# Running maxima stored by chunk and gathered by node, in the max pass of a four-layer graph network

## What is computed

```python
msgs = z[dst] @ Wd + z[src] @ Ws + edge_weight[:, None] * ww[None, :] + bm
agg = segment_max(msgs, dst)          # for each node, over its incoming edges
hidden = relu(z @ W1a + agg @ W1b + b1)
x = layernorm(z + hidden @ W2 + b2)
```

## Time and profile before

| | |
|---|---|
| median of three runs | 3843.29 us (3842.65, 3843.29, 3858.65) |
| span of the profiled execution | 3851.9 us (no other time of it is given) |
| busy in it: PE, DVE, ACT, POOL | 81%, 38%, 25%, 61% |
| first and last gather of the max pass | 1961.4 and 3185.4 us |
| granted TensorE clock over the span | 0.818 |

### The profile page before, as it was taken

The page is one execution under the profiler, slowest core; times in us unless marked ns, Lnnn a source line. Parts: engine busy times, 40 slices in busy tenths (PEclk is TensorE's granted clock), DMA queues, the critical chain, the costliest instruction groups (busy, mean ns, idle before and its releaser), DMA issues.

```text
span 3851.9 us, 54329 instructions
## 1 busy us (share of the span) xinstructions
PE 3125.2 (81%) x21070; PEld 2150.6 (56%) x21070; DVE 1459.7 (38%) x3223; ACT 958.7 (25%) x2512; POOL 2340.9 (61%) x2327
## 2 busy tenths in 40 slices
PE   3788788878889888888857787878878787999898
PEld 2444444455557677777735555555656564555454
DVE  6555555223222111111224444544444443333333
ACT  2555455122222011010122222322222232000000
POOL 3666662666662665666446666666666662777775
PEclk7899999899999999999955665665665667999899
DMA  5444444655555666666433343433444337666564
GB/s 150 162 160 166 167 149 156 200 175 185 190 181 172 193 193 188 198 193 201 144 112 103 108 116 101 119 102 112 112 127 127 111 113 253 211 226 218 195 225 144
DMA packets 278767, 621.83 MB, mean 161 GB/s; under 512 B 60077, under 2 KB 188649, under 8 KB 270953
## 3 DMA queue, kind: packets, MB, share of 16 engines
q1 hardware_dynamic: 171944, 372.56, 28.5%
...
## 4 chain that ended last, share of the span: by engine, by line
PE 56%; another core or an unknown queue 15%; issue 13%; DVE 7%; ACT 6%; DMA 3%; SPq 1%; DVEq 0%; POOL 0%; ACTq 0%; POOLq 0%
PE banks L2056 27%; PE banks L1294 5%; PE banks L2077 4%; PE banks L554 3%; PE banks L2075 3%; PE banks L1283 3%; PE banks L1272 3%; PE banks L1274 1%; PE banks L529 1%; PE banks L2170 1%; PE banks L1154 1%; DMA ring_of_rows<-weight_parts 1%; ACT arena L2363 1%; ACT arena L1213 1%
## 5 line engine op out<-in xcount | busy, mean ns | idle before, releaser
L2056 PE MATMUL banks<-arena 128*128 128x384 bf16 (+1 forms) x9310 | 1557.1, 316 | 129.0 <-issue 114.3
L2056 PEld LDWEIGHTS banks<-arena 128*128 128x128 bf16 x9310 | 914.4, 100 | 618.0 <-issue 235.8
L516 POOL DMA_INDIRECT arena<-tab_l,ring_of_rows x831 | 808.4, 973 | 472.3 <-issue 286.3
L2121 POOL DMA_INDIRECT arena<-h_pieces,span_sources x450 | 435.8, 968 | 319.2 <-issue 108.3
L2121 POOL DMA_INDIRECT ring_of_rows<-message_pieces,span_sources x396 | 430.2, 1086 | 214.1 <-issue 98.0
L2121 POOL DMA_INDIRECT ring_of_rows<-x_pieces,span_sources x306 | 332.9, 1088 | 201.3 <-PE banks L2075 101.1
L1294 PE MATMUL banks<-arena 128*128 128x64 f32 x1662 | 349.8, 380 | 123.4 <-issue 123.0
L2101 DVE TENSOR_TENSOR arena<-iota_bf,span_targets 128x768 bf16<-128x768 bf16 x243 | 134.9, 556 | 822.3 <-remote 318.3
L2121 POOL DMA_INDIRECT ring_of_rows<-l_pieces,span_sources x306 | 300.7, 983 | 233.0 <-issue 71.8
L1294 PEld LDWEIGHTS banks<-arena 128*128 128x128 f32 x1662 | 315.9, 284 | 201.5 <-issue 190.4
L1388 DVE TENSOR_TENSOR_SCAN ring_of_rows<-arena,ring_of_rows,banks 128x512 f32<-128x512 bf16 x207 | 264.2, 1277 | 135.6 <-remote 57.7
...
## 6 DMA issues: line engine op xcount, KB each, us to landing
...
arena<-scan_mask SPq DMA_DIRECT2D x208, 128.0 KB
...
arena<-tab_l,ring_of_rows POOLq DMA_INDIRECT x831
```

The source lines that it names most:

```text
L516: k.nc.gpsimd.indirect_dma_start(k.RG3[:, i % p.ring, at:at + width], None, table, bass.IndirectOffsetOnAxis(ap=k.SRC[:, i:i + 1], axis=0) ...
L2056: t = T.matmul(k.bank[i % N_SUMS][:, 0:rows.shape[-1]], counts[:, s, :], rows, start=s == 0 and n == 0, stop=s == NT - 1 and n == len(term ...
L2121: G.indirect_dma_start(k.rows[p.layer][s % n], None, k.pieces[p.layer], bass.IndirectOffsetOnAxis(ap=k.SRCG[:, at:at + 1], axis=0)).then_i ...
```

## The change

The one-hots, the selecting product and the copy of windows go. ACT now copies each turned-back chunk into one of four buffers, and SP stores it as 256 KB of DRAM, so that all running maxima lie there by edge. For each group of nodes POOL gathers the rows of the nodes' last edges from there, one indirect DMA for each tile of 128 nodes, into `BEST3`, nodes on partitions; a group's gathers stand eight chunks behind its last chunk, and behind waits for the stores of its last four chunks. Two new stages, "bturn" on PE and "bcopy" on ACT, turn them for "first". All stages of nodes move four chunks later. Turning back alternates between two banks. Which edge is a node's last is counted in the first layer: in each of the two steps of `vector_keys` two comparisons and two sums, then a few small operations (`vector_last_rows`), a small store, and at the start of `l1b` a load of 128 x 49 single words in place of the four arrays.

```diff
-HOT_RING = 3
+RUNS, NODE_CHUNKS, ROWS_AFTER = 4, 4, 8
+BACKS = (3, 0)
...
-    "l2": ("first", "relu", "second", "residual", *LN1, "xturn", "xcopy", "parts", "table", "parts2", "table2", *PIECES),
+    "l2": ("bturn", "bcopy", "first", "relu", "second", "residual", *LN1, "xturn", "xcopy", "parts", "table", "parts2", "table2",
+           *PIECES),
...
-PLACES_AT = 24
-PARKED = 2 + 5
+PARKED = 2 + 2
...
-            while done < end and (NEWEST[done] if regular else min(done, N_ET - 1)) < (c * CH if c < NCH else N_ET):
+            while done < end and (NEWEST[done] if regular else min(done, N_ET - 1)) < ((c - NODE_CHUNKS * regular) * CH if c < NCH else N_ET):
...
-def window(k, c):
-    return k.bank[c % 2][:, 0:WINDOW]
+def last_chunk(g):
+
+    return NEWEST[DONE_BY[g] - 1] // CH
+
+
+def runs_stored(k, c):
+
+    return k.sem(f"store_runs_{c % RUNS}"), 16 * (c // RUNS + 1)
+
+
+def node_rows(k, g):
+
+    return k.sem(f"node_rows_{g % 2}"), 16 * sum(GROUPS[g % 2:g + 1:2])
+
+
+def best_turned(k, g):
+    if g >= NG - 2:
+        return k.BEST_TURNED[g - NG + 3][:, 0:GROUPS[g] * P]
+    return k.BEST_TURNED[0][:, 0:GROUPS[g] * P]
 
 
 def max_tensor_l2(k, p):
     T = k.nc.tensor
 
     def node(stage, g):
-        if stage == "first":
-            T.wait_ge(*p.selected(g))
+        if stage == "bturn":
+            T.wait_ge(*node_rows(k, g))
             if g == 0:
                 T.wait_ge(k.sem("l2_folded"), 2)
             if before_group(g) >= 0:
                 T.wait_ge(*max_tabled(p, before_group(g)))
+            turn(k, g, lambda j: k.BEST3[:, j, :], H, (max_bank(g),), p.sem(stage))
+        elif stage == "first":
+            T.wait_ge(*p.at("bcopy", g))
             o = k.bank[max_bank(g)][:, 0:GROUPS[g] * P]
             T.matmul(o, k.w1_2[:, 0, :], k.ROWT3[:, gslice(g), :], start=True, stop=False)
-            T.matmul(o, k.w1_2[:, 1, :], k.BEST3[:, gslice(g), :], start=False, stop=True).then_inc(p.sem(stage), 1)
+            T.matmul(o, k.w1_2[:, 1, :], best_turned(k, g), start=False, stop=True).then_inc(p.sem(stage), 1)
...
-            T.matmul(bank[:, q * P:(q + 1) * P], k.RG3[:, i % p.ring, UP:UP + H], k.IDENT, is_transpose=True, start=i == tiles[0], stop=False)
+            T.matmul(bank[:, q * P:(q + 1) * P], k.LANDED[:, i % REGULAR_RING, :], k.IDENT, is_transpose=True, start=i == tiles[0], stop=False)
...
         T.wait_ge(k.sem("l2_scanned"), c + 1)
-        if c:
-            T.wait_ge(k.sem("l2_back_copied"), c)
+        if c >= 2:
+            T.wait_ge(k.sem("l2_back_copied"), c - 1)
         for q in range(len(chunk_tiles(c))):
-            t = T.transpose(k.bank[BACK][:, q * P:(q + 1) * P], k.SCAN[c % 2][:, q * P:(q + 1) * P], k.IDENT)
+            t = T.transpose(k.bank[BACKS[c % 2]][:, q * P:(q + 1) * P], k.SCAN[c % 2][:, q * P:(q + 1) * P], k.IDENT)
         t.then_inc(k.sem("l2_back"), 1)
-
-    def select(c):
-
-        T.wait_ge(p.hot, c + 1)
-        T.wait_ge(k.sem("l2_back_copied"), c + 1)
-        if c >= 2:
-            T.wait_ge(k.sem("l2_selected"), c - 1)
-        tiles = chunk_tiles(c)
-        for q, i in enumerate(tiles):
-            t = T.matmul(window(k, c), k.RG3[:, i % p.ring, 0:H], k.HOT[:, c % HOT_RING, q, :], start=i == tiles[0], stop=i == tiles[-1])
-        t.then_inc(p.product, 1)
...
-        if c:
-            select(c - 1)
...
-    select(NCH - 1)
...
-    def one_hots(c):
-
-        n = len(chunk_tiles(c))
-        if c >= HOT_RING:
-            V.wait_ge(p.product, c - HOT_RING + 1)
-        V.tensor_tensor(k.HOT[:, c % HOT_RING, 0:n, :], k.IOTA[:, 1:WINDOW + 1].unsqueeze(1).to_broadcast([P, n, WINDOW]),
-                        k.LOCEND[:, c * CH:c * CH + n].unsqueeze(2).to_broadcast([P, n, WINDOW]), ALU.is_equal).then_inc(p.hot, 1)
-
-    def take(c):
-
-        V.wait_ge(p.product, c + 1)
-        if c:
-            V.wait_ge(k.sem("l2_selected"), c)
-        if c % REGS == 0:
-            V.load(k.ve_regs, k.BASES[0:1, c:c + REGS])
-        V.tensor_copy(k.BEST[:, bass.ds(V.snap(k.ve_regs[c % REGS], min_val=0, max_val=N - 1), WINDOW)],
-                      window(k, c)).then_inc(k.sem("l2_selected"), 1)
...
-    V.memset(k.BEST[:, N:NP + WINDOW], 0.0).then_inc(k.sem("l2_acc_set"), 1)
-    V.wait_ge(k.sem("l2_acc_set"), 1)
     scan(0)
-    one_hots(0)
...
-            one_hots(c + 1)
...
-        if c:
-            take(c - 1)
-    take(NCH - 1)
...
+        if stage == "bcopy":
+            A.wait_ge(*p.at("bturn", g))
+            if before_group(g) >= 0:
+                A.wait_ge(*p.at("first", before_group(g)))
+            A.copy(best_turned(k, g), k.bank[max_bank(g)][:, 0:GROUPS[g] * P]).then_inc(p.sem(stage), 1)
...
-        n, slot = len(chunk_tiles(c)), c * CH % p.ring
+        n = len(chunk_tiles(c)) * P
         A.wait_ge(k.sem("l2_back"), c + 1)
-        if c * CH >= p.ring:
-            A.wait_ge(p.product, c - p.ring // CH + 1)
-        A.copy(k.RG3[:, slot:slot + n, 0:H], wide(k.bank[BACK][:, 0:n * P], P)).then_inc(k.sem("l2_back_copied"), 1)
+        if c >= RUNS:
+            A.wait_ge(*runs_stored(k, c - RUNS))
+        A.copy(k.MAXIMA[c % RUNS][:, 0:n], k.bank[BACKS[c % 2]][:, 0:n]).then_inc(k.sem("l2_back_copied"), 1)
...
+    def results(g):
+
+        if g >= 2:
+            G.wait_ge(*node_rows(k, g - 2))
+        for c in range(last_chunk(g) - RUNS + 1, last_chunk(g) + 1):
+            G.wait_ge(*runs_stored(k, c))
+        for j in gtiles(g):
+            G.indirect_dma_start(k.BEST3[:, j, :], None, k.runs_dram[0:last_chunk(g) + 1].rearrange("c p (q h) -> (c p q) h", h=H),
+                                 bass.IndirectOffsetOnAxis(ap=k.LAST[:, j:j + 1], axis=0)).then_inc(node_rows(k, g)[0], 16)
+
+    groups = list(range(NG))
     for i in range(N_ET):
+        if i % CH == 0:
+            while groups and i // CH >= last_chunk(groups[0]) + ROWS_AFTER:
+                results(groups.pop(0))
         if i >= AHEAD and i % CH == 0:
             G.wait_ge(k.sem("l2_turned"), (i - AHEAD) // CH + 1)
-        gather(k, p, i, k.tab["l2"], H, UP)
+        G.indirect_dma_start(k.LANDED[:, i % REGULAR_RING, :], None, k.tab["l2"],
+                             bass.IndirectOffsetOnAxis(ap=k.SRC[:, i:i + 1], axis=0)).then_inc(p.landed(i)[0], 16)
+    for g in groups:
+        results(g)
...
+    def store_runs(c):
+
+        S.wait_ge(k.sem("l2_back_copied"), c + 1)
+        S.dma_start(k.runs_dram[c], k.MAXIMA[c % RUNS]).then_inc(runs_stored(k, c)[0], 16)
...
+        if c:
+            store_runs(c - 1)
...
             first_slab(FIRST_SLAB_AT.index(c))
+    store_runs(NCH - 1)
     nodes(k.slots[NCH][0])
...
-    S.wait_ge(p.product, NCH)
+    for c in range(NCH - RUNS, NCH):
+        S.wait_ge(*runs_stored(k, c))
...
     V.scalar_tensor_tensor(k.WKEY[:, a:b, :], high, 2.0, rel, ALU.mult, ALU.add).then_inc(k.sem("win_keyed"), 1)
+    V.wait_ge(k.sem("win_keyed"), n + 1)
+    upto = k.WUPTO[:, 0:m].rearrange("p (s e) -> p s e", e=REC)
+    for r in range(2):
+        V.tensor_scalar(upto, rel, float(r), None, ALU.is_le).then_inc(o.sem, o.up())
+        V.wait_ge(o.sem, o.n)
+        V.tensor_reduce(k.WENDS[:, a:b, r], upto, AX_X, ALU.add).then_inc(o.sem, o.up())
+        V.wait_ge(o.sem, o.n)
+
+
+def vector_last_rows(k):
+
+    V, o = k.nc.vector, k.order
+
+    def settled():
+        V.wait_ge(o.sem, o.n)
+
+    def flat(v):
+        return v.rearrange("p s r -> p (s r)")
+
+    V.tensor_scalar(k.WFROM, k.WSTI[:, SPANS:SPANS + SETS], 2.0, -1.0, ALU.mult, ALU.add).then_inc(o.sem, o.up())
+    settled()
+    V.tensor_tensor(k.WLAST, k.WENDS, k.WFROM.unsqueeze(2).to_broadcast([P, SETS, 2]), ALU.add).then_inc(o.sem, o.up())
+    settled()
+    last, tile, at, chunk = flat(k.WLAST), k.WPARTS[0], k.WPARTS[1], k.WPARTS[2]
+    V.tensor_scalar(tile, last, 7, CH - 1, ALU.logical_shift_right, ALU.bitwise_and)
+    V.tensor_scalar(at, last, P - 1, 2, ALU.bitwise_and, ALU.logical_shift_left)
+    V.tensor_scalar(chunk, last, 9, 9, ALU.logical_shift_right, ALU.logical_shift_left).then_inc(o.sem, o.up())
+    settled()
+    V.tensor_tensor(at, at, tile, ALU.add).then_inc(o.sem, o.up())
+    settled()
+    V.tensor_tensor(chunk, chunk, at, ALU.add).then_inc(k.sem("last_rows"), 1)
...
     count_own(0)
+    vector_last_rows(k)
...
+            S.wait_ge(k.sem("last_rows"), 1)
+            S.dma_start(k.last_dram.rearrange("(s p f) -> p s f", p=P, f=4),
+                        k.WPARTS[2].rearrange("p (s f) -> p s f", f=4)).then_inc(k.sem("store_last_rows"), 16)
...
-    def places():
-
-        V.wait_ge(k.sem("park"), 16 * PARKED)
-        V.tensor_tensor(k.CHANGE, k.DST, k.NEXT, ALU.not_equal)
-        V.tensor_tensor(k.WITHIN, k.DST, k.FIRST, ALU.subtract).then_inc(o.sem, o.up())
-        V.wait_ge(o.sem, o.n)
-        V.scalar_tensor_tensor(k.LOCEND[:, 0:N_ET], k.WITHIN, 1.0, k.CHANGE, ALU.add, ALU.mult).then_inc(k.sem("l2_places"), 1)
...
```

(9 more changed lines are left out.)

19 lines of the change are left out of this document (10 added, 9 removed).

## The result

The changed kernel took 3906.23 us (median of 4 runs, 3895.66 to 3911.04) beside 3845.76 us (4 runs, 3842.65 to 3858.65): a ratio of 1.0136, 95% interval 1.0107 to 1.0166. It is slower by about 60 us where I forecast about 80 us less. The profiled execution's span is 3899.8 us, 47.9 us more than that of the kernel before.

What follows compares the result with a forecast made beforehand. The prediction took PE's work to bound the max pass, with POOL next. Pass -87, tail +2 and front +6 summed to -79 us, giving 3773 us in a profile and 3764 us as a median, range 3714 to 3818.

Steps and rivals of the forecast that it cites:

- the first reading: Max pass before the change: PE, idle 1.20 us of 5.97 a chunk, is nearest its limit and holds POOL up.
- the waits left on POOL: Max pass after the change: POOL still waits 25 us, bounds none or 168 us.
- the tail: From the last gather's end to the first load of messages: 34.3 us, not 32.7, so +2 us, bounds -3 and +8.
- the front: First layer's two key steps: extra comparisons, sums and small operations on DVE add 6 us, bounds 0 and 9.
- 875 gathers at 1.272 us: Max pass on POOL: 831 gathers plus 44 of last rows take 1113 us, against 1225 us for the pass before.
- Selection out of the chunk, PE at 3.01 us: Max pass: without the selecting product's 1.76 us, PE's chunk falls from 4.77 to 3.01 us, and POOL becomes the bound.
- The order of nodes: Node steps four chunks later: PE stands about 5.1 + 2.5 us at each group's new turn, POOL doesn't; costed at nothing.
- Stores and SP: Max pass: storing 53 MB of maxima from SP costs nothing; DMA share 0.59.
- The clock: PE in pass and tail: by the skill's rule 1.2 GHz throughout, about 3 us more; by the rows it stays.
- Rival 2: Max pass: masks, asked for only after an earlier chunk's copy, become the loop and slow it to 3909 us; chance 6%.
- Rival 3: Max pass: half the gain, as PE's late signals still cost POOL 90 us, 3829 us; chance 4%.

Runs made afterwards that it cites:

- e3: Kernel before without the selecting products on PE and their one-hots and short copies on DVE, nothing in their place: 3827.8 us, ratio 0.9936.
- e1: Changed kernel with SP's store of the maxima of chunk c-1 placed behind the load of mask c+3, not ahead: 3909.2 us, ratio 1.0147.
- e2: Changed kernel with the stores of the maxima issued by ACT behind its copy, not by SP: 3916.2 us, ratio 1.0165.
- e4: Changed kernel without the stores of the maxima and the waits on them, last rows gathered from the edges' table: 3909.0 us, ratio 1.0154.

## Why the prediction was wrong

**The step that failed** is the first reading: "PE lacks 1.20 us of 5.97, so it is the engine nearest to its limit, and it holds POOL up". PE holds POOL up, but not with its work. The 1.98 us "remote" of the earlier trace rows, at 2645.80, shows it. The product that raises `l2_turned` for it is

```profile
2640.97 0.38 PE L1274 MATMUL banks<-ring_of_rows,arena 9*128 9x512 bf16 x1
```

and the signal is on record at 2645.55, 4.20 us after that product's end. Of all that POOL stands beyond the usual 0.30 us between gathers in the pass before, 219 us, 133 lie between the end of such a product and its signal. The rest has no signal on record, or PE itself was behind; it too stands for engines that its late signals release. e3 takes 366 us of PE's work away and POOL's waits go from 186.0 to 154.7; the change takes it too, and they are 160.9. Prompt, with all of PE's work in place, they are 4.0.

With it goes the largest term of the sum, the waits left on POOL, for which I took 25 us. Reckoned as there (busy and idle time less 875 x 1.272) they are 1262.6 - 1113.0 = 149.6 us, 124.6 more. With the tail 7.8 over its term and the front 5.5 under, that is the whole distance of 127 us between the -79 of the sum and the +47.9 of the profiled executions.

**Why the lateness stays.** POOL waits when its ring is used up, that is when it has run four chunks ahead of the last `l2_turned` that reached it. Over the whole execution of the changed kernel, 78% of the signals over 3 us late arrive while POOL stands (more than 0.35 us behind its last instruction's end), though it stands only 27% of the time between their matmuls' ends and them, on average (in the kernel before 74% and 24%). That isn't only because POOL starts again on `l2_turned`: of such signals of L1154 and L1303 in the pass, for which POOL doesn't wait, 57% and 81% arrive while it stands. That, with the timeline at 2745.80, is the picture of a loop: POOL issues until it must stand, standing lets the signals out, the three engines catch up, POOL goes on. By this picture how long it takes doesn't depend on how much PE had to do. The loop is argued from these records; what is shown by edits is that without the stream of gathers there is no lateness, that more ring doesn't end it, and that less work on PE doesn't (e3).

**The other terms.**

- *875 gathers at 1.272 us.* Right: 0.975 us busy and 0.30 between. The 44 gathers of last rows in the pass cost 44 x 1.27 = 56 us, and 37.6 us came out: the waits fell by 25, and the other gathers' own time and the gaps at "issue" grew by 2 and 5. Prompt, where nothing is left to fall, 52.5 came out, and the whole change costs 2.0%.
- *Selection out of the chunk, PE at 3.01 us.* About right as work: PE is busy 3.37 us a chunk (673.24 / 1225 x 6.14), the nodes' products included, where it was 4.70. Alone it bought 21 us of the pass (e3).
- *The order of nodes.* I had PE standing some 7.6 us at each new turn, behind cover. At groups 0 to 10 POOL waited for no store (its three waits for `running_maxima` are those of the pass's end, below), so that cover held.
- *Stores and SP.* Right at nothing: without them or with them elsewhere nothing is gained (e1, e2, e4). The DMA share is 0.53, not 0.59, in a longer pass.
- *The front.* 0.5 us in the late condition and 4.0 in the prompt one, against +6 with bounds 0 and 9. The first says little: with the same front the pass starts between 1957.3 (e4) and 1968.7 us (e1).
- *The tail.* +9.8 us against +2 with bounds -3 and +8 (prompt, +3.1). The end of the pass, POOL, SP's queue and PE:

```profile
3227.74 0.94 POOL L1477 DMA_INDIRECT arena<-running_maxima,last_rows  x1 [3.25 <-DMA running_maxima<-arena]
...
3242.91 0.94 POOL L1477 DMA_INDIRECT arena<-running_maxima,last_rows  x1 [11.60 <-DMA running_maxima<-arena]
```

```profile
3262.64 0.52 SPq L1521 DMA_DIRECT2D typed_counts<-arena  x1
3268.80 7.35 SPq L3019 DMA_DIRECT2D arena<-message_pieces  x5
```

```profile
3241.50 0.90 PE L529 MATMUL banks<-consts,arena 128*128 128x128 f32 x3
```

Messages are loaded 44.3 us after the last gather's end (3224.5), against 32.7 in the earlier trace rows and the 34.3 that I reckoned. The chain through group 11's "lo" and the typed store is the one I named; its head was mis-sized, by the 10 us. The rows of group 11 start 3.3 us after the last gather and not at once, and PE turns them only at 3241.50 (L529), 17.0 us behind the last gather where I had allowed 6.3, as the turning back of the last chunk but one stands before it in PE's order.

- *The clock.* The granted clock is 0.58 in the pass, 0.61 in the earlier trace rows; behind it 0.92 and 0.94. The Trainium skill (TensorE: Matmul & The Clock Gate, HAM oscillation) tells of half rate after idle gaps; I had made of it a pass and tail wholly at 1.2 GHz. With more gaps the clock did fall a little here, but not to that level throughout. The pass didn't lose its time there: PE stood idle 45% of it.

**The rivals.** Rival 2 gave 3909 us, 3 us from the result, for a wrong reason: its sign was PE waiting for `weight_parts`, and that sign rose (29.4 us to 99.4 in all), but e1 takes two thirds of it away in the pass (93.7 to 30.4) and nothing is won. A price that fits is no proof. Rival 3, "PE's signals come late and POOL still loses 90 us to them", named the mechanism, and I gave it 4% with "little speaks for it, since POOL's slack is several chunks". Its size was off: with 161 us in place of 90 its 3829 becomes 3900, and 3906 was measured; that it comes so near is partly luck, since tail and front were off too. In the earlier trace rows the "remote" of POOL was as much evidence for it as for a busy PE; what I didn't ask is when the product of PE that released the waiting engine had ended.

In the prompt condition POOL is the bound, as the forecast had it, and the gain is still absent: POOL was the bound before the change too, so work left PE for nothing and came to the engine that had none to spare.
